# Self-attention in a decoder layer: the value products of a step issued after its last scores instead of before them

## The reference

```
q, k, v = (layernorm(x) @ W{q,k,v})          # 16 heads of 32
scores  = q @ k.T / sqrt(32), causal         # 2048 x 2048 per head and batch
attn    = softmax(scores)
mask    = clip((256 + z - dist) / 256, 0, 1) # z per head and batch
attn    = attn * mask
attn    = attn / (attn.sum(-1) + 1e-8)
out     = attn @ v
```

## Time and profile before

| what | value |
|---|---|
| median of three runs | 3192.86 us (3192.83 to 3197.88) |
| the profiled execution | 3189.68 us, span 3187.9 us |
| mean granted TensorE clock | 0.949 |
| TensorE busy | 2896.6 us (91%) |
| VectorE busy | 1853.1 us (58%) |
| ScalarE busy | 1130.8 us (35%) |
| GpSimd busy | 790.0 us (25%) |
| the self-attention's steps | from about 340 to 1715 us of the span |

### The profile page before, as it was taken

The page is one execution under the profiler, slowest core; times in us unless marked ns, Lnnn a source line. Parts: engine busy times, 40 slices in busy tenths (PEclk is TensorE's granted clock), DMA queues, the critical chain, the costliest instruction groups (busy, mean ns, idle before and its releaser), DMA issues. The chain is left out here.

```text
span 3187.9 us, 49319 instructions
## 1 busy us (share of the span) xinstructions
PE 2896.6 (91%) x18474; PEld 1645.8 (52%) x18474; DVE 1853.1 (58%) x1976; ACT 1130.8 (35%) x2670; POOL 790.0 (25%) x730
## 2 busy tenths in 40 slices
PE   7999699999999999999997899999998877777788
PEld 6877234333333334343434688888886333232345
DVE  4345498889898979888863455555554410000048
ACT  3222355555455545555552333333332101010123
POOL 0000444434344433444342122222221000000013
PEclk9999799999999999999998899999998988887889
DMA  4553767675766666666555112111212779999954
GB/s 172 182 188 132 186 140 166 136 162 135 164 143 152 154 147 143 153 148 148 124 107 182 30 63 66 66 66 66 66 66 78 275 299 421 420 420 421 420 207 161
DMA packets 215607, 555.83 MB, mean 174 GB/s; under 512 B 31534, under 2 KB 65992, under 8 KB 178585
## 3 DMA queue, kind: packets, MB, share of 16 engines
q1 hardware_dynamic: 194649, 442.24, 40.2%
q0 software_dynamic: 13824, 100.67, 16.2%
q10 hardware_dynamic: 6976, 10.75, 0.9%
HBM read 359.87 MB, written 84.14 MB: 139 GB/s over the span
## 5 line engine op out<-in xcount | busy, mean ns | idle before, releaser
L795 ACT ACTIVATE B_e<-B_pS 128x512 f32<-128x512 f32 (+3 forms) x1280 | 614.3, 533 | 611.9 <-PE B_pS L899 336.2
L749 DVE TENSOR_REDUCE mx<-B_pM 128x4 f32<-128x2048 f32 (+2 forms) x299 | 589.7, 1972 | 150.9 <-PE B_pM L885 99.5
L742 DVE SCALAR_TENSOR_TENSOR B_em_dve<-B_mask,B_e 128x1536 f32<-128x1536 f32 (+3 forms) x288 | 554.1, 1924 | 53.3 <-ACT B_e L795 47.2
L899 PE MATMUL B_pS<-B_qs,B_ks 97*128 97x512 f32 (+3 forms) x1280 | 502.4, 444 | 21.1 <-DMA B_qs<-q_hi 10.5
L695 POOL TENSOR_TENSOR B_em_pool<-B_e,B_mask 128x512 f32<-128x512 f32 (+3 forms) x288 | 385.9, 1340 | 505.3 <-ACT B_e L795 446.2
L899 PEld LDWEIGHTS B_pS<-B_qs,B_ks 97*128 97x128 f32 x1280 | 226.2, 191 | 343.2 <-issue 206.1
L933 PE MATMUL B_pD<-B_em_pool,B_ones 128*32 128x512 f32 (+3 forms) x640 | 293.4, 540 | 12.2 <-DVE B_em_dve L742 7.8
L933 PE MATMUL B_pD<-B_em_dve,B_ones 128*32 128x512 f32 (+3 forms) x1920 | 298.6, 542 | 0.0
L940 PE MATMUL B_pN<-B_em_dve,B_v 128*32 128x512 f32 (+3 forms) x1920 | 294.6, 535 | 0.0
L940 PE MATMUL B_pN<-B_em_pool,B_v 128*32 128x512 f32 (+3 forms) x640 | 290.3, 535 | 0.0
L2127 PE MATMUL E_pI<-ring,hT 128*32 128x512 f32 x1024 | 181.8, 804 | 101.4 <-DMA ring<-in_L_ffn_e_W_dram 55.2
(11 more groups left out here) (298 smaller groups left out, 5073.9 us busy)
## 6 DMA issues: line engine op xcount, KB each, us to landing
ring<-in_L_ffn_e_W_dram SPq DMA_DIRECT2D x128, 1024.0 KB, 21.9
B_e<-B_e POOLq DMA_DIRECT2D x96, 1024.0 KB, 7.7
ring<-in_L_ffn_e_Wg_dram SPq DMA_DIRECT2D x64, 1024.0 KB, 23.6
B_ks<-k_hi SPq DMA_DIRECT2D x64, 256.0 KB, 4.0
B_qs<-q_hi SPq DMA_DIRECT2D x64, 256.0 KB, 4.4
E_xq<-xT_sc ACTq DMA_DIRECT2D x18, 512.0 KB, 10.3
ring<-x_sc SPq DMA_DIRECT2D x36, 256.0 KB, 2.7
qc<-in_x_dram SPq DMA_DIRECT2D x34, 256.0 KB, 2.7
```

The lines of the kernel that those rows point to most:

```text
L742: nc.vector.scalar_tensor_tensor(em_dve[:, f % SLOTS_DVE, :, w0:], mask_of(f, mine), 1.0, e[:, f % SLOTS_E, mine, w0:], ALU.min, ALU.mult) ...
L749: nc.vector.tensor_reduce(mx[:, :, qt, c], pM[:, :, 0:w], AX.X, ALU.max).then_inc(max_taken, 1)
L795: nc.scalar.activation(e[:, f % SLOTS_E, h, w0:], pS[:, h % SBANKS, w0:], ACT.Exp, scale=SCALE).then_inc(exp_ready, 1)
L899: last = nc.tensor.matmul(pS[:, h % SBANKS, w0:], ks[0:ROWS_S, kb // NT, h, kb % NT * P:(kb % NT + 1) * P], qs[0:ROWS_S, qb, h, w0:], star ...
```

## The change

`mix` is split in two. `mix_den` has the epsilon products and the denominators and stays where `mix` was. `mix_num` has the values, with the waits that belong to them (`v_loaded`, `num_out`), and raises `mixed` as before; it is issued after the scores of heads 2 and 3. TensorE's step becomes: scores 0 and 1, denominators, turn, scores 2 and 3, values, unit. Operands, semaphores and all other engines' programs stay as they are.

```diff
-            def mix(f):
+            def weighed(f):
+                return [em_pool[:, f % SLOTS_POOL, h, width(f):] if h < POOL_HEADS else
+                        em_dve[:, f % SLOTS_DVE, h - POOL_HEADS, width(f):] for h in range(HPG)]
+
+            def mix_den(f):
                 w0 = width(f)
                 it, row = f // STEPS, row_at(f)
                 qb, kb = FLAT[f % STEPS]
                 first, final = kb == 0, kb == NT * (qb + 1) - 1
-                if kb == NT * qb:
-                    pe.wait_ge(v_loaded[qb], 16 * (it + 1))
                 if first:
                     at_least(pe, den_out, row)
...
+            def mix_num(f):
+                w0 = width(f)
+                row = row_at(f)
+                qb, kb = FLAT[f % STEPS]
+                first, final = kb == 0, kb == NT * (qb + 1) - 1
+                if kb == NT * qb:
+                    pe.wait_ge(v_loaded[qb], 16 * (f // STEPS + 1))
                 if first:
                     at_least(pe, num_out, row)
                 for h in range(HPG):
                     cols = slice(h * DH, (h + 1) * DH)
-                    last = nc.tensor.matmul(pN[cols, w0:], v[:, kb, cols], weighed[h],
+                    last = nc.tensor.matmul(pN[cols, w0:], v[:, kb, cols], weighed(f)[h],
                                             start=first, stop=final, tile_position=(0, h * DH))
                 last.then_inc(mixed, 1)
...
                 if f < ITS * STEPS:
                     scores(f, (0, 1))
-                mix(f - 2)
+                mix_den(f - 2)
                 if (u - 1) % STEPS in ENDS and EARLY < u <= ITS * STEPS:
                     turn(row_at(u - 1))
                 if f < ITS * STEPS:
                     scores(f, (2, 3))
+                mix_num(f - 2)
                 if u < ITS * STEPS:
                     unit(u)
```

More of the change, by code:

```diff
@@ L926, in mix @@
                     opened = True
-                weighed = [em_pool[:, f % SLOTS_POOL, h, w0:] if h < POOL_HEADS else em_dve[:, f % SLOTS_DVE, h - POOL_HEADS, w0:]
-                           for h in range(HPG)]
                 pe.wait_ge(masked_pool, f + 1)
@@ L932, in mix @@
                     cols = slice(h * DH, (h + 1) * DH)
-                    nc.tensor.matmul(pD[cols, w0:], ones[:, :], weighed[h],
+                    nc.tensor.matmul(pD[cols, w0:], ones[:, :], weighed(f)[h],
                                      start=not opened, stop=final, tile_position=(0, h * DH))
                     opened = opened or h == HPG - 1
+            def mix_num(f):
[5 more added lines that the diff above has]
+                    pe.wait_ge(v_loaded[qb], 16 * (f // STEPS + 1))
                 if first:
```

## The result

The changed kernel takes 3246.7 us (median of four runs, 3242.8 to 3249.7) against 3192.9 of the kernel before in the same comparison: 1.0169 times as long, 95% interval 1.0149 to 1.0189. The forecast was 3236, in a range of 3205 to 3270. The profiled execution took 3242.8, span 3241.0, so it is set against 3189.7 and 3187.9: 53.1 us more.

What follows compares the result with a forecast made beforehand. It took TensorE as the bound, partly waiting for exponentials, with VectorE nearly as full. Terms -5 +7 +12.5 +21.5 +13.5 -6 gave +43.5 on 3189.7, so 3233.2; with 3.2 for the median, 3236, range 3205 to 3270.

Steps and rivals of the forecast that it cites:

- Second step of a row, den copy: Steps where ScalarE's den copy waits for the later values, without a turn: 0.78 us more, 16 times, plus 12.5.
- With a turn: Second steps of a row with den copy and transposition of the maxima: 1.43 us more, 15 times, plus 21.5.
- The turn alone: Tenth steps of third and fourth rows: values no longer fill TensorE's wait for VectorE; 0.9 us, 15 times, plus 13.5.
- Full steps: Undisturbed full steps, twelve a round in eight rounds: 3.90 us against 3.95, minus 5 in all.
- scores to N costs 0.43, as scores to D does: TensorE's full step: price from the last score to the values, put at 0.43 where scores to unit costs 0.33.
- the forecast 0.97: TensorE's full step: price from values to unit, absent from the trace, taken from the nearest change of tile shape.
- The estimate of 1.03 for N to unit: TensorE, values to unit, by the Trainium skill's drain of about 175 ns; over 299 units the sum 19 us larger.
- Even a faster TensorE would win little there: A pair of full steps: VectorE nearly as full, 8.76 us against TensorE's 8.77.
- Narrow steps: Narrow steps and the first of a row: 0.05 us lost to tile shape, 17 steps by eight, plus 7.
- The last 19 steps: Steps without units: values cover the wait for exponentials, a full one 3.46 us against 3.97; minus 6 in all.
- price of the switch: Rivals on N to unit: dearer, 1.08, 3269 us, chance 0.14; cheaper, 0.86, 3205 to 3220, chance 0.10.
- The delays: Rivals, 46 den copy or turn steps: VectorE's lateness absorbs delays; wholly, faster, 0.06; three quarters, 3187 to 3199, 0.06.

Runs made afterwards that it cites:

- e1: The changed kernel with a semaphore of its own for the denominators, on which only the den copy waits; 3209.0 us, 1.0060 of the kernel before.
- e3: The changed kernel with the new order only on the 46 steps with a den copy or a turn; 3259.3 us, ratio 1.0212.
- e2: The changed kernel with the new order only on the 274 steps without den copy or turn; 3198.5 us, ratio 1.0012.
- e9: Kernel before, with new order only on full steps without den copy or turn, denominators' own semaphore, keys of blocks 1 and 2 loaded at step 38; 3159.4 us.
- e11: e2 with the keys of blocks 1 and 2 for the next round loaded at step 38; 3180.0 us, ratio 0.9960.
- e7: The kernel before with the denominators' own semaphore and one load of keys issued two steps later; 3202.7 us, ratio 1.0038.
- e10: The kernel before with the denominators' own semaphore and the keys of blocks 1 and 2 loaded at step 38; 3183.1 us, ratio 0.9967.

## Why the prediction was right, point by point

**The forecast** was +43.5 us on the profiled execution, by six terms; +53.1 was measured there, +53.8 on the medians.

*Second step of a row, den copy:* predicted 0.78 a step and 12.5 in all, measured 0.81 on step 13 and 11.3. Head 3, N, den copy and exponential 2 were put at 1.73, 2.15, 2.62 and 3.11; the trace has 1.73, 2.16, 2.66 and 3.15. Right, and e1 and e3 show the cause.

*With a turn:* predicted 21.5, measured 25.9. Den copy 3.88 and maxima copy 4.37 as put; unit 4.88 against 4.89; next step 5.35 against 5.36. The mechanism is exact in that round; the term was too small because in 10 of the 15 steps the clock fell before their end, and the last products ran at the lower level (steps of up to 6.5 us).

*The turn alone:* predicted 13.5, measured 8.9. Step 21 has 0.63 in the median, not 0.9. The price was right and a gain was left out. Step 181 before and the same step of the changed kernel, 80 later:

```profile
1114.59 0.45 PE L899 MATMUL B_pS<-B_qs,B_ks 97*128 97x384 f32 x1
...
1118.14 0.28 PE L868 MATMUL B_pM<-ident,B_mm 128*16 128x128 f32 x1 [0.44 <-DVE B_mm L753]
...
1119.45 0.36 PE L899 MATMUL B_pS<-B_qs,B_ks 97*128 97x256 f32 x1
```

```profile
1507.76 0.45 PE L899 MATMUL B_pS<-B_qs,B_ks 97*128 97x384 f32 x1
...
1511.02 0.28 PE L868 MATMUL B_pM<-ident,B_mm 128*16 128x128 f32 x1 [1.30 <-DVE B_mm L753]
...
1513.25 0.36 PE L899 MATMUL B_pS<-B_qs,B_ks 97*128 97x256 f32 x1
```

From the turn to the next step it is 2.23 instead of 1.31, 0.92 more. But VectorE has the maxima ready 0.29 earlier in the step (3.26 instead of 3.55). In step 33 the median even fell by 0.18; two of its seven ran into the lower clock and took 7.24 and 7.27, and they give half of the 8.9. e1 and e2, which keep and undo the new order there, have 75.9 and 63.0. In e2, with values ahead of the turn there, these steps are even faster than before.

*Full steps:* the step that failed. I put 3.90 and it was 3.76. The term "scores to N costs 0.43, as scores to D does" read a wait as a price. In the changed kernel scores to D and scores to N take 0.32 (0.34 after the first score, then 0.66 to D), no more than the unit's 0.33. The 0.43 of the earlier trace rows belonged to the product that had waited for its bank. The opposite direction, 32-column tiles to anything else, was put right: 0.11. D to scores takes 1.00 where D to N took 0.89, both behind scores, and 0.97 where it took 0.85 behind epsilon products. The 1.00 instead of the forecast 0.97 is the other difference in these rows: D or N directly behind scores takes 0.03 to 0.04 longer. The drain that the Trainium skill states in TensorEngine Tiling (Array Packing), section Key Properties, shows in this trace as 0.11 to 0.12 us on leaving the 32-column tiles, and as those 0.03 to 0.04 on entering them. The estimate of 1.03 for N to unit was as near as the 0.97. By terms the step is 0.34+0.32+1.00+0.34+0.32+1.00+0.44 = 3.76.

*"Even a faster TensorE would win little there"* was wrong. The two steps take 8.37 us, below the 8.76 that I had as its bound. The bound was not one: VectorE's weighing of step 178 took 2.38 us with GpSimd's mask running beside its first 0.75 us (1102.42 to 1104.00, weighing from 1103.26). Here, with 0.26 beside it, it takes

```profile
1497.01 1.88 DVE L742 SCALAR_TENSOR_TENSOR B_em_dve<-B_mask,B_e 128x1536 f32<-128x1536 f32 x1
```

This is the same all through the stage. A full weighing with no mask beside it, or with one that started after it, took 1.74 to 1.76 us in both traces (83 and 87 of them). One that began while the mask ran was longer by nearly the rest of the mask: 2.41 with 0.78 of it, 2.78 with 1.17. In this step the mask starts 1.31 us in where it started at 1.61, and the weighing at 2.63 instead of 2.45, so less of the mask is left. VectorE even idles 0.22 us before its third reduction.

*Narrow steps:* 0.05 was too little; 0.13 to 0.14 on steps 0, 3, 11, 23, 37 and 39 (medians of e2 or of the changed kernel against before). Full and narrow together were put at plus 2; they gave minus 13.6. The full steps gave minus 24.5, of which 11.4 are at steps 7 and 30, where the kernel before had long steps in some rounds; the others gave plus 10.9.

*The last 19 steps:* predicted minus 6, measured minus 4.9. Most clean ones are 3.32 where I had 3.46. Against that stand the last turn (0.35), the last den copy (0.79) and the step behind it (1.17).

*Not predicted:* the steps behind a stalled one, plus 21.6, and step 34, plus 7.0. The first is the clock: in all 15 rounds the step behind the stalled one overlaps a stretch at the lower level, and over the stage TensorE spends 106 us at it where it spent 27. The prediction has no term for that; I never asked what a stall of 2.5 us does to the steps after it. Step 34 is the late sum that e2 shows, and the prediction put the DMAs at nothing.

So the direction and the main mechanism were right, and that the total came out within 10 us is in part luck. 28.6 us had no term, and the steps with a turn gave 4.4 more than forecast. Against that, full and narrow steps came out 15.6 us below their terms and the turn alone 4.6. The errors cancelled in part.

**The rivals.** Neither price of the switch held: N to unit is 1.00, near the value taken. The delays were not absorbed: VectorE's reductions, which follow the delayed unit, waited in turn. On the page of the profile, the third column of the group is the idle time ahead of them; it was 150.9 us before:

```profile
L749 DVE TENSOR_REDUCE mx<-B_pM 128x4 f32<-128x2048 f32 (+2 forms) x299 | 590.5, 1975 | 238.1 <-PE B_pM L885 170.3
```

## What to carry to other kernels

Before moving work behind other work, list every wait on its semaphore and what stands behind each waiter in its own queue: here one copy in front of two exponentials cost 38 us of 54, and a second semaphore gave them back. Move only where the cover is needed (full steps; e9 is 20.6 us below e11, which moves the narrow ones too but also lacks the semaphore), and leave work ahead of a known wait (turns) where it fills the hole. When an order gets faster, look at transfers that were late without harm before; moving one by two steps only moves the stall, and it has to go where nothing is in flight.

## What the hardware showed that I had not expected

Behind the stalls of 1.40 and 1.07 us in step 245 the granted clock was 0.68 in the next step, and its denominators started 0.86 us apart instead of 0.45. All 15 such pairs of steps met the lower clock. In e1 the stall of 1.40 us stands alone in these steps: in 11 of 15 rounds a step of 3.82 us at full speed followed, as in step 246. In two more the clock fell within the stalled step itself. In the last two it fell right behind it: the first step 5 took 4.21 us like the others, and step 6 took 5.37 at 0.68. So the stalls make the lower clock likelier; no length of a stall in these traces decides it. Over steps 6 and 26 the lengthening is 21.6 us, two fifths of the loss. TensorE: Matmul & The Clock Gate of the Trainium skill, in Loop structure matters more than you think, says that a long wait for a DMA between matmuls lets the array drop to half clock. These rows agree as to the direction, with two shorter waits for other engines. But e11's long steps 26 came behind steps 25 of 4.10 us, the length of before.

A sum of 1 MB by DMA landed 12.5 us after its issue behind four loads of 256 KB, and after about 7.0 where the loads of keys were elsewhere (e7, e10; one load of v at most was under way).

VectorE's full weighing took 1.75 us, and longer by nearly the rest of GpSimd's mask when it began while that ran; a mask that began after it did not lengthen it.
